# A decoder layer on one core: the order of roundings, remainders and the exponential in its second attention

## What is computed

```python
x = _layernorm(x + _L0_attn_ref(x, L0_attn_Wq, L0_attn_Wk, L0_attn_Wv, L0_attn_Wo), axis=-1)
x = _layernorm(x + _L0_xattn_ref(x, ctx_4096, ctx_4096, pos_BxS2, mask_BxSxS2_ik0, L0_xattn_Wq, ...), axis=-1)
x = _layernorm(x + _L0_ffn_ref(x, L0_ffn_weight, L0_ffn_bias, L0_ffn_centroids, L0_ffn_assignments), axis=-1)
```

```python
q = (query @ Wq).reshape(nb, q_len, H, D).transpose(0, 2, 1, 3)      # H, KVH, D = 32, 8, 128
k = (key @ Wk).reshape(nb, q_len, KVH, D).transpose(0, 2, 1, 3)
v = (value @ Wv).reshape(nb, q_len, KVH, D).transpose(0, 2, 1, 3)
q = q * cos + _rotate_half(q) * sin                                   # rotary embedding, k alike
scores = jnp.where(mask == 0, -1e9, jnp.einsum('bhqd,bhkd->bhqk', q, k) / sqrt(D))
x = jnp.einsum('bhqk,bhkd->bhqd', jax.nn.softmax(scores, axis=-1), v)
return x.transpose(0, 2, 1, 3).reshape(nb, q_len, H * D) @ Wo
```

## Time and profile before

| | |
|---|---|
| median of three runs | 802.83 us |
| time of the profiled execution | 803.76 us |
| its span, first to last instruction | 801.6 us |
| TensorE busy | 760.9 us, 95% |
| VectorE busy | 596.9 us, 74% |
| POOL busy | 401.3 us, 50% |
| ScalarE busy | 322.1 us, 40% |
| mean granted TensorE clock | 0.99 of 2.4 GHz |

### The profile page before, as it was taken

How to read it: one execution, slowest core, us unless ns; L and a number is a source line. 1 busy time by engine, 2 the same in 40 slices (tenths; PEclk the granted TensorE clock), 3 DMA queues, 4 the chain that set the end, 5 groups by cost and what they waited for, 6 DMA issues and landing times.

```text
span 801.6 us, 13879 instructions
## 1 busy us (share of the span) xinstructions
PE 760.9 (95%) x4809; PEld 650.8 (81%) x4809; DVE 596.9 (74%) x1143; ACT 322.1 (40%) x684; POOL 401.3 (50%) x381
## 2 busy tenths in 40 slices
PE   6889999989989999999999999999999999999996
PEld 4777777779878887888888888888888888888875
DVE  4778888877777676777677667766766777688777
ACT  4455555563333333242333324233333323334335
POOL 7656666674644554444446444444644544445303
PEclk9799999999999999999999999999999999999999
DMA  7710003012352222322222232222233222131002
GB/s 182 190 35 18 16 16 121 3 56 54 71 141 80 53 59 60 103 71 52 78 52 52 71 105 60 52 78 52 52 76 106 54 53 79 27 102 31 1 1 105
DMA packets 107875, 53.54 MB, mean 67 GB/s; under 512 B 80449, under 2 KB 96961, under 8 KB 107841
## 3 DMA queue, kind: packets, MB, share of 16 engines
q1 hardware_dynamic: 107008, 51.51, 25.1%
q10 hardware_dynamic: 576, 1.05, 0.4%
q0 software_dynamic: 256, 0.52, 0.3%
HBM read 32.62 MB, written 2.10 MB: 43 GB/s over the span
## 4 chain that ended last, share of the span: by engine, by line
PE 69%; DVE 15%; issue 5%; POOL 4%; ACT 2%; DMA 2%; SPq 1%; DVEq 0%; POOLq 0%; ACTq 0%
PE bank L743 19%; PE bank L678 16%; PE bank L494 10%; DVE arena_r L1611 5%; PE s_bank L757 4%; PE bank L549 3%; PE s_bank L759 2%; PE bank L727 2%; PE bank L575 2%; DVE small L1699 2%; PE bank L901 2%; DVE arena_f L1693 1%; PE s_bank L727 1%; ACT arena_r L1010 1%; PE s_bank L599 1%
## 5 line engine op out<-in xcount | busy, mean ns | idle before, releaser
L743 PE MATMUL bank<-arena_r 128*128 128x512 f32 x768 | 191.5, 398 | 0.0
L1010 ACT ACTIVATE arena_r<-bank 128x256 fp32r<-128x256 f32 (+2 forms) x249 | 105.0, 459 | 214.4 <-PE bank L710 84.7
L678 PE MATMUL bank<-arena_r 128*128 128x512 f32 x720 | 185.2, 400 | 2.9 <-POOL arena_r L1454 2.4
L743 PEld LDWEIGHTS bank<-arena_r 128*128 128x128 f32 x768 | 139.7, 188 | 26.9
L678 PEld LDWEIGHTS bank<-arena_r 128*128 128x128 f32 x720 | 130.6, 188 | 32.2 <-POOL arena_r L1454 2.8
L494 PE MATMUL bank<-arena_r 128*128 128x256 f32 (+1 forms) x1056 | 147.7, 296 | 2.4 <-DVE arena_r L1611 1.6
L494 PEld LDWEIGHTS bank<-arena_r 128*128 128x128 f32 x1056 | 138.1, 192 | 9.7 <-DVE arena_r L1611 2.2
L1611 DVE TENSOR_TENSOR arena_r<-bank,arena_r 128x256 fp32r<-128x256 f32 (+2 forms) x217 | 99.6, 485 | 54.1 <-ACT arena_r L1010 53.8
L1010 ACT ACTIVATE arena_r<-arena_f 128x512 fp32r<-128x512 f32 (+2 forms) x178 | 104.6, 637 | 58.6 <-DMA arena_f<-arena_f 45.5
L1611 DVE TENSOR_TENSOR arena_r<-arena_f,arena_r 128x512 fp32r<-128x512 f32 (+1 forms) x95 | 87.4, 929 | 16.9 <-ACT arena_r L1010 16.9
L1445 POOL TENSOR_TENSOR arena_f<-arena_f 128x512 f32<-128x512 f32 x30 | 39.2, 1306 | 115.5 <-DVE arena_f L1780 115.4
(11 more groups left out here) (164 smaller groups left out, 1187.1 us busy)
## 6 DMA issues: line engine op xcount, KB each, us to landing
arena_f<-arena_f SPq DMA_DIRECT2D x120, 128.0 KB, 2.5
arena_f<-in_L_xattn_Wo SPq DMA_DIRECT2D x8, 1024.0 KB, 5.4
arena_f<-in_L_xattn_Wq SPq DMA_DIRECT2D x14, 512.0 KB, 4.0
arena_f<-in_x SPq DMA_DIRECT2D x8, 256.0 KB, 3.0
arena_f<-in_x SPq DMA_DIRECT2D x1, 2048.0 KB, 10.2
arena_f<-in_L_xattn_Wk SPq DMA_DIRECT2D x8, 256.0 KB, 3.0
arena_f<-in_L_xattn_Wv SPq DMA_DIRECT2D x8, 256.0 KB, 3.3
arena_f<-in_ctx SPq DMA_DIRECT2D x8, 256.0 KB, 3.3
```

What stands on the lines that cost most here:

```text
L678: mm = pe.matmul(BQ2[f][:], w2q_s[a][:, e, j, f, :], xT[b][:, e, tok], start=(e == 0 and n == 0), stop=(e == EC - 1 and n == 2))
L743: mm = pe.matmul(BO2[i][:], at2[a][:, h, i * P:(i + 1) * P], w2o_s[b][:, h, :], start=(h == 0 and n == 0), stop=(h == HG - 1 and n == 2))
L1010: act.activation(dst, src, ACT.Copy).then_inc(done, 1)
```

## The change

Three edits of order; no instruction is added, removed or altered in itself.

- ScalarE: `exponents(u)` stands right behind `corrections(u)` (and the context roundings, where there are any), ahead of the two `q_high` of the next unit. In units 0 to 2 the order is as before.
- VectorE: `total2(u)` stands ahead of both `q2_low` of the next unit; before, one was ahead of it and one behind. In units 0 to 2 the order is as before.
- POOL: in unit 0, `wq_low(1, 0)` and `wq_low(1, 1)` stand ahead of `sum_q(3)`.

The first two edits reach 26 units (3 to 28), among them seven with c = 0 (4, 8, 12, 16, 20, 24, 28).

```diff
--- before.py
+++ after.py
@@ -1188,12 +1188,10 @@
                 if turns_ctx(u + 1):
                     ctx_high(2 * c1)
                     ctx_high(2 * c1 + 1)
-                    exponents(u)
+                exponents(u)
                 if kv_next:
                     q_high(u + 1, c1, 0)
                     q_high(u + 1, c1, 1)
-                if not turns_ctx(u + 1):
-                    exponents(u)
                 if c == 0:
                     if starts_with(u):
                         act.wait_ge(s_wo, T)
@@ -1489,11 +1487,11 @@
                     sum_q(2)
                 if is_unit(u + 1):
                     sum_k(u + 1)
-                if is_unit(u + 3):
-                    sum_q(u + 3)
                 if starts_with(u):
                     wq_low(1, 0)
                     wq_low(1, 1)
+                if is_unit(u + 3):
+                    sum_q(u + 3)
                 if split and c == 1:
                     wq_low(g + 1, 2)
                     wq_low(g + 1, 3)
@@ -1881,12 +1879,9 @@
                 if turns_ctx(u + 1):
                     ctx_low(2 * c1)
                     ctx_low(2 * c1 + 1)
-                elif kv_next:
+                total2(u)
+                if kv_next:
                     q2_low(u + 1, c1, 0)
-                total2(u)
-                if turns_ctx(u + 1):
-                    q2_low(u + 1, c1, 0)
-                if kv_next:
                     q2_low(u + 1, c1, 1)
                 if starts_with(u):
                     rope2_q(2, 1, 0)
```

## The result

The changed kernel took 807.92 us (median of nine runs, 802.42 to 811.08), the kernel before in runs on the same chip and shown with it 804.32 us. The ratio on record is 1.0057, with a 95% interval of 1.0035 to 1.0079: some 4.6 us slower (the two medians by themselves differ by 3.6). The profiled execution's span is 806.8 us against 801.6.

The account below looks back on a forecast made before the run. TensorE was taken as the bound, matmul after matmul with two visible waits in the second attention; -1.9 - 1.7 + 3.9 = +0.3 us gave 804.1 on 803.76, 803.1 on the median, forecast 803.6, range 799.5 to 811.5.

Parts of the forecast that it names:

- Part 1: Units 0 and 1: POOL's `wq_low` pair ahead of `sum_q(3)` removes TensorE's 2.4 us stall; -1.9 us, bounds 0 and 2.4.
- Part 2: ScalarE, units 3 to 28: exponential ahead of `q_high` removes TensorE's wait in unit 5, -1.7 us; other units cost nothing.
- third rival: Unit 5's late landing is an accident of this execution: +2.0 on the median, 804.8 us; chance 0.12.
- Part 3: VectorE, units 3 to 28: `total2` ahead of `q2_low` costs zero in c = 1, 2, 3, and +3.9 us over seven c = 0 units.
- the lock won: In c = 0 units VectorE's `wo_low(g, 2)` goes ahead of POOL's second `wo_low`; forecast cost 0.55 us per unit.
- I take 0.55: Cost in us per c = 0 unit, assuming VectorE's `wo_low(g, 2)` asks 0.05 us before POOL's first `wo_low` ends.
- second rival: In c = 0 units POOL's second `wo_low` goes before VectorE's `wo_low(g, 2)`: 1.25 us more per unit, 812.4 us; chance 0.2.
- first rival: The `q2_low` remainder costs nothing in c = 0 units, leaving gains of -3.6 us: 800.2 or 799.2 us; chance 0.2.
- the fourth: Late landings are common in other runs, so the early exponential gains 2 to 8 us more: 795 or less; chance 0.03.

Follow-up runs that it names:

- odd quarters: The changed kernel with the new ScalarE and VectorE order only in c = 1 and c = 3 units; 799.95 us, ratio 0.9950 to the kernel before.
- not in c = 0: The changed kernel with the order of before kept in c = 0 units only; 798.55 us, ratio 0.9939 to the kernel before.
- `wo_low` behind `p2_low`: The changed kernel with VectorE's `wo_low(g, 2)` moved behind `p2_low` in c = 0 units; 801.09 us, ratio 0.9976 to the kernel before.
- POOL's second apart: The changed kernel with POOL's second `wo_low` moved behind `sum_k(u + 1)` in c = 0 units, except unit 0; 803.20 us, ratio 0.9982.
- the real delay: The changed kernel with two one-column VectorE instructions ahead of `wo_low(g, 2)` in units 4, 8, ... 28; 812.51 us, ratio 1.0122.
- the increments: The changed kernel with three empty VectorE semaphore increments ahead of `wo_low(g, 2)` in c = 0 units; 807.59 us, ratio 1.0038.

## Why the prediction was right, and which step was off

The forecast of no change within 799.5 to 811.5 held the time, and 0.57% is within the 1% that I had called the same. It held by the width of the range, not by the sum: the slowdown is clear of no change by its interval, and my sum said +0.3 us, not +4.6. By steps:

- **Part 1** (-1.9): measured -1.70 in the profile of the change, -1.73 alone. `pv(1)` came at 238.14, or 237.2 without the later start of the stage, for a forecast of 237.0. The landing that I couldn't see was the limit there. In six others (odd quarters, not in c = 0, `wo_low` behind `p2_low`, POOL's second apart, the real delay, the change once more) unit 1 took 18.36 or 18.37 us, and units 0 and 1 were 2.6 shorter than before: there `pv(1)` did not wait for the landing. That is not a larger gain of the edit. `q_high(2)` waits for the DMAs behind `sum_q(3)` and starts 4.5 us behind their first issue in every profile, so it moves with `sum_q(3)`, and that with VectorE's `rope2_q(3)`, which itself waits for the DMAs of query 2. These came late in the kernel before and in the change, and early in the six. `rope2_q(3)` before, then in the change once more (19.25 and 18.03 us into the stage):

```profile
223.16 0.69 DVE L1779 TENSOR_TENSOR arena_f<-bank,arena_f 128x512 f32<-128x512 f32 x1 [1.26 <-DMA arena_f<-arena_f]
```

```profile
219.43 0.69 DVE L1777 TENSOR_TENSOR arena_f<-bank,arena_f 128x512 f32<-128x512 f32 x1
```

  The VectorE edit alone has POOL's old order and had the early landing, at 18.11, and there the wait that Part 1 removes was half as long:

```profile
232.13 3.02 PE L678 MATMUL bank<-arena_r 128*128 128x512 f32 x12 [1.29 <-POOL arena_r L1454]
```

  Late landing against late, the edit is worth 1.70 us (42.27 and 40.57 for units 0 and 1); early against early 1.52 (41.15 and 39.63). The POOL edit alone had a unit 0 of 22.09 us, 0.8 longer; the ScalarE edit alone, which leaves POOL as it was, had one of 22.04, and the pair differs by 1.71 (42.25 and 40.54). Why those DMAs land early or late is open.
- **Part 2**, unit 5 (-1.7): measured -1.73. The third rival, that its landing is an accident, falls: it was there at 5.9 to 6.0 us in the profile before and in the change, and the unit is at 19.32 with the POOL edit alone.
- **Part 3**, c = 1, 2, 3: no cost, as said, for a slack of hundredths (17.40 to 17.54 in the change).
- **Part 3**, c = 0, the lock won: +0.55 predicted per unit, and +0.50 to +0.59 measured in the four units that won, with `wo_low(g, 2)` at 0.68 where I had 0.65. The chain up to its request grew by 1.46 us in unit 24 (from 7.47 to 8.93 behind `corrections`), for the 1.45 predicted. With POOL's second `wo_low` away, where none is lost, the seven units take 3.90 us more than before, which is the +3.9 of the sum.
- **The step that failed** is "I take 0.55, as VectorE's request, by this count, comes 0.05 us ahead": I made one value for seven units of a margin that is below what the records resolve (0.02 us by the rows of POOL's second apart). The mechanism was right, and the term of +3.9 was too small: it measured +7.3 in the change's profile. What the runs show is a mixture. 3 of 7 lost in the change's profile, 1 of 7 in its second, 3 of 7 with the increments, 2 of 7 with the VectorE edit alone, 0 of 7 with POOL's second `wo_low` away, 7 of 7 with the request 0.12 us later. A loss costs 1.1 to 1.2 us on top (predicted 1.25): 19.25 against 18.1. The second rival had the mechanism and named the in-between case; its full price, seven units, came only when it was forced. The first rival, that c = 0 units pay nothing, falls with every profile of the change. Of the fourth, that late landings are common and pay more than once, no profile shows anything: only units 1 and 5 became shorter.

An estimate of the usual cost follows from the four profiles with an open race (the change twice, the increments, the VectorE edit alone): 9 losses in 28 units are 2.25 an execution at 1.15 us, and 3 of the 9 were followed by half clock at 1.6 us. 3.9 + 2.6 + 1.2 - 1.6 - 1.7 is +4.4 us, beside the measured +4.6.

In the profile of the change the 5.2 us close: -1.70 - 1.73 + 7.31 + 0.32 = +4.2 in the stage, and 0.94 from ahead of it. For this last one the granted clock (third column from the end; the first is the stretch) of the kernel before and then of the changed one in the first stretches:

```profile
10.00:20.00 10.00, 5.48 (x33) 4.11 (x31) 6.31 (x12) 5.16 (x10) 7.00 (x8) 0.89 0.71 116
20.00:30.00 10.00, 9.98 (x56) 8.43 (x56) 4.90 (x8) 4.68 (x9) 5.29 (x5) 0.60 0.98 284
30.00:40.00 10.00, 6.80 (x47) 5.78 (x45) 9.38 (x20) 4.87 (x8) 8.54 (x9) 0.83 0.43 97
```

```profile
10.00:20.00 10.00, 6.35 (x34) 5.09 (x32) 5.44 (x10) 3.55 (x7) 7.48 (x8) 0.77 0.82 118
20.00:30.00 10.00, 9.08 (x40) 7.58 (x40) 5.68 (x10) 4.94 (x10) 4.00 (x4) 0.55 1.00 283
30.00:40.00 10.00, 6.98 (x53) 6.12 (x53) 8.47 (x19) 5.35 (x10) 8.48 (x9) 0.83 0.34 77
```

TensorE was at a mean of 0.77 and 0.55 of full speed where it had been at 0.89 and 0.60. No edit reaches that part, and the other profiles of this study start the stage between 201.3 and 205.9 us. I take it for scatter; what makes the clock come up earlier or later there wasn't tried.

## What to carry to other kernels

An instruction that fills an engine's wait is free where it stands, and moving it behind the wait puts its full length, and its lock conflicts, on the chain: ask unit by unit whether there is slack, and move it only where the wait ends elsewhere (here by a DMA, in c = 1 and 3). Where two edits on two engines exchange the order of the same pair of steps, try them together and apart: here each alone cost twice what both cost. If a sum rests on who asks first by hundredths of a microsecond, carry both outcomes and their mixture, or take the race away.

## What the runs showed of the hardware that I had not expected

**The outcome of the lock is open at a tie.** With VectorE's request 0.02 us or so ahead of the end of POOL's first instruction, the same program wins or loses from unit to unit. The Trainium skill (SBUF — State Buffer, Who interferes with whom) has it that whoever issues first gets the shared pair (the SBUF ports that VectorE and POOL have in common) for a whole instruction; the length of each outcome agrees with that, 0.68 or 1.82 us. That it can go either way in one program is what the runs add.

**A wait of 1.8 us can cost nearly as much again.** In the increments' run TensorE waited 1.8 us in unit 16. Its stretches in that unit (busy time of the engines, third from the end the granted clock):

```profile
498.00:502.00 4.00, 2.54 (x16) 1.93 (x15) 4.00 (x8) 1.04 (x3) 2.66 (x2) 1.00 0.00 0
502.00:503.00 1.00, 0.68 (x10) 0.68 (x12) 1.00 (x3) 0.01 (x1) 0.73 (x1) 1.00 0.00 0
504.00:506.00 2.00, 2.00 (x7) 1.53 (x6) 1.27 (x3) 0.14 (x1) 0.00 (x0) 0.50 0.00 0
508.00:509.00 1.00, 1.00 (x6) 0.84 (x5) 0.00 (x0) 0.00 (x0) 1.00 (x2) 1.00 0.00 0
```

The clock is 1.00 through the wait, and 0.50, which is the 1.2 GHz level, in 504 to 506, and the unit took 20.87 us instead of 19.25. The same wait in unit 8 of the change left the clock alone:

```profile
361.00:363.50 2.50, 1.03 (x5) 0.50 (x3) 2.50 (x5) 0.11 (x1) 1.14 (x2) 1.00 0.00 0
363.50:367.00 3.50, 3.20 (x23) 2.67 (x24) 3.32 (x7) 1.54 (x5) 0.72 (x1) 1.00 0.00 0
```

Of the sixteen losses of the lock in five profiles, four were followed by half clock (unit 4 of the real delay and of the VectorE edit alone, 16 and 20 of the increments), at 1.5 to 1.6 us each. What tells them apart wasn't found.

**VectorE's semaphore increments did not hold the engine**: in unit 16 they were carried out 2.8 us ahead of the instruction that they were written in front of. Two one-column instructions did hold it, for 0.12 us together.
